# Down-projection in three groups instead of two, with the next unit's first transposes between the second and the third

## The reference

```python
x = x + layernorm(attn(layernorm(x)))   # dilated attention: each head takes every 4th position of a
                                        # 512 segment; softmax over those positions of q.k, times V; @ Wo
x = x + layernorm(ffn(layernorm(x)))    # gate, up: 1024 -> 3072 (int weights / 127);
                                        # h = silu(gate) * up; down: 3072 -> 1024
```

## Time and profile before

| | us |
|---|---|
| median of 2 runs | 3764.5 (3760.7 to 3768.3) |
| the profiled execution | 3763.8 |
| its span, first to last instruction, slowest core | 3762.3 |
| spans of the 8 cores | 3733.2 to 3762.3 |
| busy: TensorE matmuls | 2711.2 (72%) |
| busy: DVE / ACT / POOL | 1101.6 / 759.8 / 459.4 |

### The profile page before, as it was taken

How to read it: one execution, slowest core, us unless ns; L and a number is a source line. 1 busy time by engine, 2 the same in 40 slices (tenths; PEclk the granted TensorE clock), 3 DMA queues, 4 the chain that set the end, 5 groups by cost and what they waited for, 6 DMA issues and landing times.

```text
span 3762.3 us, 36322 instructions; the slowest of 8 cores (3733.2 to 3762.3 us)
## 1 busy us (share of the span) xinstructions
PE 2711.2 (72%) x12867; PEld 1274.1 (34%) x12867; DVE 1101.6 (29%) x1972; ACT 759.8 (20%) x1441; POOL 459.4 (12%) x373
## 2 busy tenths in 40 slices
PE   0123679955996669955997679955996679955996
PEld 0122334322442334422443334322442334422442
DVE  1121331234213431244213421244113431244213
ACT  0000321123111321123112321123111321123111
POOL 2110100112002100122002200121002100121002
PEclk9999789976998689976998689976998689976998
DMA  7887312441226212450226212450226212450224
GB/s 146 175 154 147 115 38 86 127 165 33 73 81 208 86 34 84 129 169 33 73 81 203 91 40 84 133 164 29 75 85 204 84 34 81 131 172 30 73 86 133
DMA packets 197136, 392.50 MB, mean 104 GB/s; under 512 B 42808, under 2 KB 55120, under 8 KB 192352
## 3 DMA queue, kind: packets, MB, share of 16 engines
q1 hardware_dynamic: 156608, 295.76, 25.3%
q0 software_dynamic: 40352, 94.43, 10.8%
HBM read 356.57 MB, written 60.82 MB: 111 GB/s over the span
## 4 chain that ended last, share of the span: by engine, by line
PE 60%; DVE 13%; DMA 10%; ACT 8%; issue 5%; POOL 2%; DVEq 0%; ACTq 0%; SPq 0%; POOLq 0%
PE pg L702 18%; PE pu L708 17%; PE pd L768 16%; DMA ring_d<-scr_d 3%; ACT xh_tm L215 2%; PE ptr L224 2%; DMA xhB<-wg 2%; POOL x_tm L456 2%; PE pkv L402 2%; PE pao L615 2%; DMA xhB<-wu 2%; DVE y_sb L781 1%; PE pq L402 1%; DMA scr_d<-h_sb 1%; DMA qkvo<-wo 1%
## 5 line engine op out<-in xcount | busy, mean ns | idle before, releaser
L702 PE MATMUL pg<-xhB,ring_g 128*128 128x512 bf16 x3072 | 751.8, 389 | 7.6 <-DVE xhB L231 7.6
L768 PE MATMUL pd<-ring_d,h_sb 128*128 128x512 bf16 x3072 | 694.0, 386 | 69.1 <-DMA ring_d<-scr_d 32.8
L708 PE MATMUL pu<-xhB,ring_u 128*128 128x512 bf16 x3072 | 726.8, 379 | 0.0
L724 DVE TENSOR_TENSOR h_sb<-silu_sb,pu 128x512 bf16<-128x512 f32 x384 | 264.2, 688 | 1092.6 <-ACT silu_sb L719 1092.6
L719 ACT ACTIVATE silu_sb<-pg 128x512 f32<-128x512 f32 x384 | 229.3, 597 | 1129.2 <-PE pu L708 1129.2
L768 PEld LDWEIGHTS pd<-ring_d,h_sb 128*128 128x128 bf16 x3072 | 299.5, 99 | 463.6 <-issue 128.6
L702 PEld LDWEIGHTS pg<-xhB,ring_g 128*128 128x128 bf16 x3072 | 306.8, 100 | 387.1 <-issue 43.3
L708 PEld LDWEIGHTS pu<-xhB,ring_u 128*128 128x128 bf16 x3072 | 301.3, 98 | 365.4 <-issue 5.5
L825 POOL TENSOR_TENSOR ostg<-t_sb,x_tm 128x1024 f32<-128x1024 f32 x64 | 150.3, 2348 | 2125.3 <-ACT t_sb L817 2113.5
L224 PE MATMUL ptr<-identb,xh_tm 128*128 128x128 bf16 x1024 | 106.1, 269 | 398.6 <-ACT xh_tm L215 394.7
L402 PE MATMUL pkv<-xhB,qkvo 128*128 128x256 bf16 x1024 | 178.4, 349 | 75.6 <-ACT k_sb L490 71.4
(11 more groups left out here) (79 smaller groups left out, 1439.4 us busy)
## 6 DMA issues: line engine op xcount, KB each, us to landing
ring_d<-scr_d SPq DMA_DIRECT2D x384, 256.0 KB, 2.9
ring_g<-scr_g SPq DMA_DIRECT2D x192, 256.0 KB, 2.6
ring_u<-scr_u SPq DMA_DIRECT2D x192, 256.0 KB, 3.0
x_tm<-x POOLq DMA_DIRECT2D x64, 512.0 KB, 7.2
qkvo<-scr_q SPq DMA_DIRECT2D x32, 1024.0 KB, 5.6
qkvo<-scr_q SPq DMA_DIRECT2D x64, 512.0 KB, 6.2
out<-ostg POOLq DMA_DIRECT2D x64, 512.0 KB, 4.1
scr_q<-qkvo SPq DMA_DIRECT2D x4, 2048.0 KB, 7.3
```

What stands on the lines that cost most here:

```text
L702: P.op("tensor", lambda t, slot=slot, gsl=gsl, nt=nt, kcc=kcc, pg=pg: t.matmul(pg[:, 512 * gsl:512 * gsl + 512], ring_g[:, D * slot + 128 ...
L708: P.op("tensor", lambda t, slot=slot, gsl=gsl, nt=nt, kcc=kcc, pu=pu: t.matmul(pu[:, 512 * gsl:512 * gsl + 512], ring_u[:, D * slot + 128 ...
L724: P.op("vector", lambda v, gsl=gsl, ssl=ssl, hc=hc, nt=nt, pu=pu: v.tensor_mul(h_sb[:, D * hc + 512 * nt:D * hc + 512 * nt + 512], silu_sb ...
L768: P.op("tensor", lambda t, ji=ji, j=j, hf=hf, kcc=kcc, slot=slot, pd=pd: t.matmul(pd[ji][:, 512 * hf:512 * hf + 512], h_sb[:, D * kcc + 12 ...
```

## The change

- One PSUM tile `ptr2` of two banks is allocated for the whole kernel. It takes the place of `p_tr0`/`p_tr1` of the prologue, of `ptr{u}` and of `ptr_{u}`.
- The down-projection runs in **three groups**: slices (0, 1, 2), (3, 4, 5), (6, 7), with three `pd` tiles (6 banks) in place of four. Each group goes over all 24 chunks, so `ring_d` is filled 72 times a unit instead of 48. Matmuls and casts keep their number.
- The next unit's x statistics follow each group, for that group's slices: 0 to 2 after group 0, 3 to 5 after group 1, 6 and 7 after group 2. The batch step `rst1a` (slices 0 to 3) comes after those of group 1, and behind it, still ahead of group 2, the tiles 0 to 3 of the next unit: ACT apply, transposes, DVE copies. `rst1b` comes after the statistics of group 2, at the end of the down-projection.
- At the start of a unit those tiles and statistics are gone; Q and K of rr = 0 come first and wait for the last casts (`b2yevac`). In unit 0 the four tiles stand ahead of Q and K.

The core of the diff:

```diff
+        ptr2 = E(nc.psum_tensor("ptr2", [128, 2048], BF16))
...
                 def emit_qk_mm(rr, u=u, pq=pq, pkv=pkv):
                     si = (u * 4 + rr) % 2
+                    if rr == 0:
+                        P.wait("tensor", vc, M.get(("b2yevac", u - 1), 0))
...
-                for j in (0, 1):
-                    emit_xhat_tile(j, ptrU, M[("rst1a", u)], M.get(("b1_done", u - 1), 0), b2war)
+                    for j in (0, 1, 2, 3):
+                        emit_xhat_tile(j, ptr2, M[("rst1a", 0)], 0)
                 emit_qk_mm(0)
                 load_wqk(2)
-                for j in (2, 3):
-                    emit_xhat_tile(j, ptrU, M[("rst1a", u)], M.get(("b1_done", u - 1), 0), b2war)
-                if u > 0:
-                    for j in (4, 5, 6, 7):
-                        emit_ln1_stats(j)
-                    M[("rst1b", u)] = emit_batch_rstd(MV, 4, 8)
...
+            b2groups = ((0, 1, 2), (3, 4, 5), (6, 7))
             with contextlib.ExitStack() as pctx:
                 pd = [pctx.enter_context(nc.psum_tensor(f"pd{u}_{i}", [128, D], F32))
-                      for i in range(4)]
-                for grp in range(2):
+                      for i in range(3)]
+                for grp, g_slices in enumerate(b2groups):
...
-                    if u + 1 < n_units and grp == 0:
-                        for ji in range(4):
-                            emit_ln1_stats(ji)
-                        M[("rst1a", u + 1)] = emit_batch_rstd(MV, 0, 4)
+                    if u + 1 < n_units:
+                        for j in g_slices:
+                            emit_ln1_stats(j)
+                        if grp == 1:
+                            M[("rst1a", u + 1)] = emit_batch_rstd(MV, 0, 4)
+                            for j in (0, 1, 2, 3):
+                                emit_xhat_tile(j, ptr2, M[("rst1a", u + 1)],
+                                               M[("b1_done", u)])
+                        elif grp == 2:
+                            M[("rst1b", u + 1)] = emit_batch_rstd(MV, 4, 8)
```

More of the change, by code:

```diff
@@ L282, in build_nc @@
             M[("scrq", rr)] = 32 * ((rr // 2) + 1)
-        with nc.psum_tensor("p_tr0", [128, D], BF16) as p_tr0, \
-             nc.psum_tensor("p_tr1", [128, D], BF16) as p_tr1:
-            p_tr = (p_tr0, p_tr1)
+        if True:
+            p_tr = (ptr2[:, 0:1024], ptr2[:, 1024:2048])
             for wsi, (w_src, w_scr, w_key) in enumerate(
@@ L353, in build_nc @@
             nbase = 2 * half
-            with nc.psum_tensor(f"ptr{u}", [128, 2048], BF16) as ptrU, \
-                 contextlib.ExitStack() as pctx:
+            with contextlib.ExitStack() as pctx:
                 pq = pctx.enter_context(nc.psum_tensor(f"pq{u}", [128, 512], F32))
@@ L559, in build_nc @@
                         if rr < 2:
-                            b2war = M.get(("b2yevac", u - 1), 0)
                             for j in (4 + 2 * rr, 5 + 2 * rr):
-                                emit_xhat_tile(j, ptrU, M[("rst1b", u)],
-                                               M.get(("b1_done", u - 1), 0), b2war)
+                                emit_xhat_tile(j, ptr2, M[("rst1b", u)],
+                                               M.get(("b1_done", u - 1), 0))
                         if rr + 3 < 4:
@@ L750, in build_nc @@
                             P.wait("sync", tc, M[(u, grp, kcc - 4)])
-                        elif grp == 1 and kcc < 4:
-                            P.wait("sync", tc, M[(u, 0, HCN - 4 + kcc)])
+                        elif grp > 0 and kcc < 4:
+                            P.wait("sync", tc, M[(u, grp - 1, HCN - 4 + kcc)])
                         elif u > 0 and grp == 0 and kcc < 4:
@@ L760, in build_nc @@
                         P.wait("tensor", drd[slot])
-                        if kcc == 0:
+                        if kcc == 0 and grp == 0:
                             P.wait("tensor", vc, h_ready_v)
-                        for ji in range(4):
-                            j = 4 * grp + ji
-                            if kcc == 0 and grp == 1:
-                                P.wait("tensor", vc, M[("yevac", ji)])
+                        for si2, j in enumerate(g_slices):
+                            if kcc == 0 and grp > 0:
+                                P.wait("tensor", vc, M.get(("yevac", si2), 0))
                             for hf in range(2):
-                                P.op("tensor", lambda t, ji=ji, j=j, hf=hf, kcc=kcc, slot=slot, pd=pd: t.matmul(
-                                    pd[ji][:, 512 * hf:512 * hf + 512],
+                                P.op("tensor", lambda t, si2=si2, j=j, hf=hf, kcc=kcc, slot=slot, pd=pd: t.matmul(
+                                    pd[si2][:, 512 * hf:512 * hf + 512],
                                     h_sb[:, D * kcc + 128 * j:D * kcc + 128 * j + 128],
@@ L772, in build_nc @@
                                     start=(kcc == 0), stop=(kcc == HCN - 1)),
-                                    tc if (ji == 3 and hf == 1) else None)
+                                    tc if (si2 == len(g_slices) - 1 and hf == 1) else None)
                         M[(u, grp, kcc)] = tc.n
-                        if grp == 1 and kcc >= HCN - 4:
+                        if grp == 2 and kcc >= HCN - 4:
                             M[("ring_d", kcc)] = tc.n
                     dn_done_t = tc.n
-                    for ji in range(4):
+                    for si2, j in enumerate(g_slices):
@@ L779, in build_nc @@
                         P.wait("vector", tc, dn_done_t)
-                        P.wait("vector", ac, M.get(("ln4apply", 4 * (grp - 1) + ji), 0))
-                        P.op("vector", lambda v, ji=ji, pd=pd: v.tensor_copy(
-                            y_sb[:, D * ji:D * ji + D], pd[ji][:]), vc)
-                        M[("yevac", ji)] = vc.n
-                    if grp == 1:
+                        P.wait("vector", ac, M.get(("ln4applyp", si2, grp - 1), 0))
+                        P.op("vector", lambda v, si2=si2, pd=pd: v.tensor_copy(
+                            y_sb[:, D * si2:D * si2 + D], pd[si2][:]), vc)
@@ L785, in build_nc @@
+                        M[("yevac", si2)] = vc.n
+                    if grp == 2:
                         M[("b2yevac", u)] = vc.n
-                    for ji in range(4):
-                        j = 4 * grp + ji
+                    for si2, j in enumerate(g_slices):
                         jsl = j % 2
                         mvp, ltp, rsp, nmp = MV2P(jsl), LT2P(jsl), RS2P(jsl), NM2P(jsl)
-                        P.wait("vector", vc, M[("yevac", ji)])
+                        P.wait("vector", vc, M[("yevac", si2)])
@@ L821, in build_nc @@
                         M[("ln4apply", j)] = ac.n
+                        M[("ln4applyp", si2, grp)] = ac.n
                         P.wait("gpsimd", ac, M[("ln4apply", j)])
```

27 lines of the change are left out of this document (12 added, 15 removed).

## The result

| | before | after |
|---|---|---|
| median of the runs, us | 3762.9 (10 runs) | 3985.9 (11 runs) |
| ratio to before, with 95% interval | | 1.0604 [1.0575, 1.0634] |
| profiled execution / its span, us | 3763.8 / 3762.3 | 3986.5 / 3985.0 |
| DMA bytes of the core, MB | 392.5 | 442.9 |

The changed kernel is 6.0% slower. In some executions of some kernels the cores of one die or both ran at a lower clock; the ratios, and all times but the two medians of this table, leave these out. The forecast was 3900 us in a range of 3845 to 3965: the direction is right, the size is not, and the time lies above the range.

The account below looks back on a forecast made before the run. TensorE was taken to bound the kernel. Each boundary's terms summed to 156.5 us against 136.3, +20.2; seven times +141.4, with -5.6 for the last unit, on 3763.8 gave 3900 us, range 3845 to 3965.

Parts of the forecast that it names:

- Group 0: First down-projection group: 144 matmuls at 0.2167 us, 31.2 us, ring loads covered.
- Group 1 and its start: Second down-projection group: 31.2 us of matmuls, 4.7 lost at its start, 6.5 of ring waits, 42.4 us in all.
- ring term: Waits for ring_d weight loads: 6.5 us in group 1, 2.0 in group 2, 1.5 in the last unit's group 2.
- the lower clock: In group 2, after the long wait, TensorE starts at granted clock 0.50: 2.2 us added (0 to 2.2).
- T1 to group 2: From group 1's last matmul to group 2's first, queued behind the moved transposes and slice 5's x load: 33.9 us.
- Group 2: Last down-projection group: 20.8 us of matmuls, 2.2 for the clock, 2.0 for the ring, 25.0 us in all.
- T2 to V: From the down-projection's end to the next unit's V matmuls: 24.0 us, x landing 5.7, Q and K lying inside.
- Last unit: Down-projection and tail without x loads: 112.8 us instead of 118.4, so -5.6 us.
- B: Rival: the ring paces group 2, landing 4.7 us, group 2 36.8 us instead of 25.0, 3983 us; chance 10%.
- A: Rival: stages interleave as hoped, transposes ready by group 1's casts, stall 4.7 us not 33.9, about 3680 us; chance 2%.
- C: Rival: no measurable difference, with x loads landing at 3.9 us and group 2 starting warm, 3834 us; chance 5%.
- The signs named: Profile after: `xh_tm` wait about 29 us, `k_sb` 10 to 16, Q and K 3 to 6 after down-projection, `ring_d` some 65, +50 MB.

Follow-up runs that it names:

- eight slots: The changed kernel with eight 256 KB slots instead of four for the down-projection's weights (ring_d plus idle ring_g): 1.0299, 3873 and 3876 us.
- the load was moved: The changed kernel with the load of rr = 2's Q and K weights behind rr = 0's V matmuls and x load 7: 1.0514, 3960 us.
- three groups alone: The changed kernel with the moved tiles and x statistics back where the kernel before has them, only the three groups kept: 1.0264, 3861 us.
- interleaved two-group kernel: Kernel before, with tiles 0 to 3 behind group 1's casts, slices 6 and 7's chains behind V, statistics 4 to 7 ahead of their tiles: 0.9741, 3664 us.
- the fastest kernel: Kernel before with two groups, tiles and chains interleaved, and eight ring_d slots instead of four: 3620 and 3622 us in two executions.

## Why the prediction was right in kind and wrong in size

**Group 0, 31.2 predicted:** 31.7, with 0.4 of ring waits on the mean; with eight slots it is 31.2.

**Group 1 and its start, 42.4 predicted:** 44.4, the 1.5 us hole ahead of it included. The ring term was right (6.5 taken, 6.6 measured). With eight slots the ring waits fall by 4.1 but the group by 6.0, so the ring waits cost more than themselves. The starts of the matmuls show where the other 2 us lie (six cores, seven boundaries). 1.5 are matmuls that follow each other at 0.43 instead of 0.2167 us, the lower clock: 2.6 us of them in the changed kernel, 1.1 with eight slots, at a mean granted clock of 0.92 and 0.97 over the group. 0.3 are the start after each wait. What is left with eight slots, 38.4 - 31.2 - 2.5 = 4.7, is the start that was predicted.

**T1 to group 2, 33.9 predicted:** 33.9, the mean of six cores. (On the other two, the records of the first matmuls of group 2 are missing.) The parts agree as well: 19.4 to the x load of slice 5, 5.4 for its landing (mean of all cores; 5.7 taken), 4.7 from first to last transpose. What was read from the order of the instructions came out to the microsecond, and the run with the transposes behind group 2 shows that this order was the cause.

**Group 2, 25.0 predicted, 29.7 measured (63.6 - 33.9; 29.5 on the six cores alone): this step failed, +4.7 a boundary.** The term that was mis-sized is the ring term: 2.0 us taken, 5.5 measured. "2.6 + 0.2 + 0.87 = 3.67 against 3.47 for four steps gives 1.2 us over six rounds ... I take 2.0". The form of the term fits, its landing does not. The 2.6 was the landing of group 0, where one load leaves every 1.73 us. Here one would have to leave every 0.87 us, and with the waits one left every 1.2 us. The landing in that stretch of the changed kernel was:

```profile
DMA to landing us min/median/max: 2.5/3.4/4.6
```

With 3.4 the same formula gives 3.4 + 0.2 + 0.87 = 4.47 against 3.47, times six is 6.0; measured were 5.5 us of ring waits. Besides, the ring waits again cost more than themselves. In an unbroken row a matmul starts 0.2167 us after the one before, but the last one ahead of a wait takes its full 0.38 us in the trace. With nearly nine ring waits a group, and a few shorter ones, that makes 1.7 us, which the working did not have, while the lower clock cost 1.3 us where 2.2 were taken.

The landing was longer where loads left more often (medians over all cores and boundaries, loads 9 to 22 of a group): 2.6 us at one per 1.73 us in group 0 before, 3.0 at one per 1.30 us in group 0 after, 3.5 at one per 1.2 us in group 2, and 3.9 at one per 0.88 us in group 2 with eight slots. So the shortened step seems to have worked against the cover twice: less time to hide in, more to hide. The rate of issue is not all of it: in the last unit, where the output stores of group 1 run beside group 2 and no x load does, the landing was 4.1 us at one per 1.44 us, with 275 GB/s at a share of 0.92 from 3943 to 3960 of core 3. There group 2 took 30.6 us on core 3, with eight ring waits between 0.2 and 1.4 us. Group 0 after moves 180 GB/s at a share of 0.63 against 139 at 0.47 before:

```profile
1127.00:1158.00 31.00, 30.58 (x142) 13.90 (x143) 0.28 (x1) 0.00 (x0) 0.00 (x0) 1.00 0.63 180
```

The Trainium skill, "DMA: Bandwidth & Descriptors", section Bandwidth, had served for an estimate near zero for this term: below 75% of peak, so under 326 GB/s, still leaves room for 302. That is an upper bound and doesn't say that the rate is reached. The trace agrees only with eight slots, where 249 GB/s were moved in the window and no wait was left; with four slots, at 194 GB/s, the bandwidth did not bound, but how many loads were under way and how long each took. Whether the longer landing comes from the core's own loads or from the other cores, which stream the same stretch at the same time, no run here tells.

**T2 to V, 24.0 predicted, 26.5 measured: +2.5.** I took x landing as 5.7, as before the change, and costed no new neighbour; measured were 8.0. "Q and K (6 us, even with a wait for weights) lie inside" was true of their own time; what they set off was left out. The step of the working that was missing is to ask what an earlier instruction frees, and who loads into it. The 24.0 came out exactly once the load was moved.

**Last unit, -5.6 predicted, +3.3 measured: 9 us.** Here the ring term of group 2 was taken as 1.5, where 5 to 8 us were lost in the cores I read. It is the same error as in group 2. Predicted were 112.8 us in all and measured 120.6; group 2 with its start is 5.7 of that and group 1 1.5. (The 36.4 for group 1 holds 0.5 us that its terms, 31.2 and 4.7, do not give.) The last microsecond is that the stretch before takes 117.4 us on the mean of the cores and not the 118.4 of the slowest. With eight slots it is 109.6, so that the shorter tail does bring what was written, and more.

**The sum.** Predicted per boundary 156.5, measured 166.3: 4.7 from group 2, 2.5 from x landing, 2.0 from group 1, 0.5 from group 0. Seven times 9.8 is 69, with the last unit 78, of the 86 us between 3900 and 3986. Of the rest, 4 are that the slowest core lies 15.4 us above the mean of the cores now (3985.0 and 3969.6) and lay 11.4 above it before (3762.3 and 3750.9); some 3 are the gate and up stage, and 2 that a boundary took 136.0 us before on the mean, not the 136.3 of the one that I read.

**The rivals.** B, the ring pacing group 2, was priced at 3983. That the time is so close to it is luck: B assumed 36.8 us for group 2 with a landing of 4.7, measured are 29.7 with 3.5, and the rest of the time came from T2 to V, group 1 and the last unit. Where x loads run beside group 2 (three groups alone) it does take 38 to 39. So the measured term lies between my value and the rival's; I took mine from the landing at the slower issue rate and stopped the range at 3965, short of the rival. A, the hoped-for interleaving, failed on the queue order as stated. By the rule of the Trainium skill, "Perfetto Trace Analysis", section Optimization Strategy, interleaving regimes may gain; this change, which did it in the wrong order of the queue, lost 6.0%, and the runs agree where nothing ready stands behind a late input, with 2.6% less time for the interleaved two-group kernel and some 3.8% less with eight slots. C is refuted.

**The signs named.** The `xh_tm` wait of about 29 us (30.2 in the first boundary) and the `k_sb` wait of 10 to 16 us (15.3 on the mean of seven) are there. Q and K start 5.8 us after T2 on the mean. The bytes rose by the 50 MB written. `ring_d` waits were to rise to 65 and rose to 100: the one named sign that points at the failed term, together with "or if group 2 took over 30 us", which it does in some boundaries.

**Left open.** What makes the landing longer, the core's own issue rate, its stores or the other cores; what paces the ring beside x loads with eight slots (6.5 to 6.8 us of waits); the interval of the fastest kernel.

## What to carry to other kernels

Before moving an instruction with a late input ahead of others in an in-order queue, list what is queued behind it: here 96 ready matmuls stood 34 us behind 32 transposes, and that line of the working was exact. Size a ring as landing under the new issue rate against slots times the new step, not by the landing in the old, slower stretch; using each load for fewer matmuls shortens the cover, and here the landing grew as well. And for every instruction that comes earlier, follow the buffer it frees and the semaphore it shares: the next load starts earlier too, and may meet the one on the path.

## What the runs showed of the hardware

- The landing of a 256 KB load was longer in the busier stretches: median 2.6 us at one per 1.73 us (139 GB/s moved), 3.0 us in group 0 after (180 GB/s), 3.4 us in group 2 with four slots (194 GB/s).
- One stream of 256 KB loads moved 194 GB/s with four slots and waits, 249 GB/s with eight slots and none, 288 GB/s at a DMA share of 0.93 in its fullest 17 us.
- x loads of 512 KB: the two behind group 2 land in 5.7 us on the mean when the weight load of 1 MB waits for them, and in 8.0 beside it; those of slices 3 to 5 land in 5.5 us while TensorE waits and the ring stands still, and in 9.2 beside the back-to-back ring of group 2 (10.8 to 13.2 in the boundary shown).
- A wait costs more than its length where the clock is lower after it: 16 transposes take 2.14 us after the hole of 30.23 us, at a granted clock of 0.50 (1.2 GHz), and 1.05 us where they start 1.48 us after the last matmul, at 1.00 (2.4 GHz).
